# A block-wise FP4 quantiser on VectorE: the rounding constant from one ScalarE activation, in a decoder layer on one core

## What is computed

```
scale = max(max(|x| in the block) / 6, 1e-12)
xn    = x / scale
q     = grid[searchsorted(mid, |xn|)] * sign(xn) * scale
grid  = 0, 0.5, 1, 1.5, 2, 3, 4, 6      mid = 0.25, 0.75, 1.25, 1.75, 2.5, 3.5, 5
ffn   = down_q @ quant(silu(gate_q @ quant(x)) * (up_q @ quant(x)))
```

## Time and profile before

| what | value |
|---|---|
| time, median of 3 runs | 622.29 us (620.88 to 623.05) |
| the profiled execution's own time | 618.94 us |
| its span, first to last instruction | 617.2 us |
| PE busy | 549.6 us, 89% |
| DVE busy | 512.0 us, 83%, in 1444 instructions |
| ACT busy | 285.8 us, 46% |
| POOL busy | 177.5 us, 29% |
| mean granted clock of TensorE | 0.972 of full speed |

### The profile page before, as it was taken

The page is one execution under the profiler, slowest core; times in us unless marked ns, Lnnn a source line. Parts: engine busy times, 40 slices in busy tenths (PEclk is TensorE's granted clock), DMA queues, the critical chain, the costliest instruction groups (busy, mean ns, idle before and its releaser), DMA issues.

```text
span 617.2 us, 16429 instructions
## 1 busy us (share of the span) xinstructions
PE 549.6 (89%) x5724; PEld 351.0 (57%) x5724; DVE 512.0 (83%) x1444; ACT 285.8 (46%) x671; POOL 177.5 (29%) x251
## 2 busy tenths in 40 slices
PE   3686898889999999999999998998999998899875
PEld 2554354546565666666576656564665765455543
DVE  3587888787889989898999997567989996887894
ACT  1342145466454555545545455454455554444412
POOL 7014141423132414233242413141232424211211
PEclk9998699899999999999999998798999999998999
DMA  8366553445453554536263636345452635330000
GB/s 253 80 187 186 157 154 110 146 124 139 138 147 95 128 165 110 168 102 186 72 180 106 170 90 179 107 124 157 112 170 77 171 102 153 88 89 16 26 8 26
DMA packets 75933, 77.14 MB, mean 125 GB/s; under 512 B 13068, under 2 KB 67404, under 8 KB 75852
## 3 DMA queue, kind: packets, MB, share of 16 engines
q1 hardware_dynamic: 73612, 73.75, 42.1%
q10 hardware_dynamic: 2240, 2.35, 1.3%
HBM read 39.89 MB, written 27.00 MB: 108 GB/s over the span
## 4 chain that ended last, share of the span: by engine, by line
PE 50%; DVE 29%; issue 9%; ACT 4%; DMA 4%; SPq 2%; POOL 2%; DVEq 0%; POOLq 0%; ACTq 0%
PE misc L2248 16%; PE misc L2234 7%; DVE junk L1431 4%; PE prob L2173 4%; PE score L2164 3%; PE xpv L2223 3%; PE prob L2179 3%; PE apv L2211 3%; PE misc L2289 3%; DVE amax L1423 2%; DVE xden L1470 2%; DVE qt L1348 2%; PE misc L2276 2%; DVE qt L1338 2%; PE score L2140 2%
## 5 line engine op out<-in xcount | busy, mean ns | idle before, releaser
L1431 DVE CUSTOM_DVE_ANT_0 junk<-score,maskbias 112x375 bf16<-112x375 f32 x256 | 128.8, 541 | 27.3 <-PE score L2164 26.4
L932 ACT ACTIVATE xP<-prob 128x448 f32<-128x448 f32 (+1 forms) x192 | 94.0, 541 | 54.4 <-PE prob L2179 53.9
L2248 PE MATMUL misc<-wguT,xqT 128*128 128x352 f32 x224 | 80.8, 489 | 1.9 <-ACT xqT L892 1.1
L741 POOL TENSOR_TENSOR move_a<-mT,eye 128x448 bf16<-128x448 bf16 x32 | 36.3, 1152 | 73.6 <-ACT mT L892 73.6
L2164 PE MATMUL score<-xK,xQ 64*128 64x375 f16 x256 | 52.0, 339 | 5.8 <-DVE xmax L1431 2.6
L765 POOL TENSOR_TENSOR rstd<-veps,half 128x1 f32<-128x1 f32 (+1 forms) x44 | 28.2, 640 | 96.7 <-DVE veps L1506 96.7
L761 POOL TENSOR_TENSOR aattT<-anum,aden 128x224 f32<-128x224 f32 x16 | 11.1, 693 | 155.0 <-DVE aden L1470 107.9
L2248 PEld LDWEIGHTS misc<-wguT,xqT 128*128 128x128 f32 x224 | 39.4, 193 | 25.8 <-issue 9.0
L741 POOL TENSOR_TENSOR move_x<-mT,eye 128x448 bf16<-128x448 bf16 x32 | 33.1, 1040 | 72.0 <-ACT mT L892 72.0
L2223 PE MATMUL xpv<-xP,xV 128*32 128x112 f32 (+1 forms) x1536 | 51.5, 268 | 0.5 <-ACT xP L932 0.3
L2248 PE MATMUL misc<-xwvT_s,ctxT_s 128*128 128x256 f32 (+1 forms) x192 | 49.9, 392 | 1.5 <-ACT kcf L892 1.1
(11 more groups left out here) (158 smaller groups left out, 1095.5 us busy)
## 6 DMA issues: line engine op xcount, KB each, us to landing
xk_dram<-xk_parts SPq DMA_DIRECT2D x64, 192.0 KB, 3.2
xK<-xk_dram SPq DMA_DIRECT2D x16, 768.0 KB, 4.6
ctxT_s<-in_ctxT SPq DMA_DIRECT2D x15, 375.0 KB, 3.7
aq_dram<-aq_parts SPq DMA_DIRECT2D x64, 64.0 KB, 2.5
ak_dram<-ak_parts SPq DMA_DIRECT2D x64, 64.0 KB, 2.4
aQ<-aq_dram SPq DMA_DIRECT2D x16, 256.0 KB, 2.9
aK<-ak_dram SPq DMA_DIRECT2D x16, 256.0 KB, 2.9
xq_dram<-xq_parts SPq DMA_DIRECT2D x64, 64.0 KB, 2.1
```

Source lines behind the costliest of these rows:

```text
L741: pool.tensor_tensor(dst[:, big], mT[:, n, big].rearrange("p (j q) -> p j q", j=2).unsqueeze(2).to_broadcast([P, 2, GH, HS]), eye[:].unsqu ...
L932: act.activation(xP[0:KEYS[c], g % 2, c], prob[m][0:KEYS[c], 0:GH * S].rearrange("p (h q) -> p h q", h=GH), ACT.Exp).then_inc(probs.taken[ ...
L1431: dve.tensor_tensor_reduce(junk[:, m], score[m][0:S, 0:SC], maskbias[:], 1.0, -3.0e38, ALU.add, ALU.max, xmax[:, b.par, h // (2 * GH), h / ...
L2248: mm = pe.matmul(misc[m][0:rows_, 0:cols], actT(c), weightT(c), start=(c == 0), stop=(c == DT - 1))
```

## The change

The rounding constant no longer comes from two VectorE steps. After the product (k = 3) ScalarE writes the absolute value of it, times 2^22, as bf16 into `qt2`. VectorE then takes the maximum with a floor and adds or subtracts in the same instruction, so k = 4 is the addition, k = 5 the subtraction, k = 6 the product with the scale: seven steps for nine. The factor for ties moves into the product of k = 3, the sign is turned back in the last step. Step 4 waits for ScalarE (`turned()`), not for the step before it.

```
-                    done(dve.tensor_tensor(blocks(t1), blocks(v), spread(r), ALU.mult))
+                    done(dve.scalar_tensor_tensor(out=blocks(t1), in0=blocks(v), scalar=TIE, in1=spread(r), op0=ALU.mult,
+                                                  op1=ALU.mult))
                 elif k == 4:
-                    done(dve.tensor_scalar(t2.bitcast(U16), t1.bitcast(U16).rearrange("p (n k) -> p n k", k=2)[:, :, 1],
-                                           0x7F80, None, ALU.bitwise_and))
+                    done(dve.scalar_tensor_tensor(out=t1, in0=t2, scalar=FLOOR, in1=t1, op0=ALU.max, op1=ALU.add))
                 elif k == 5:
-                    done(dve.tensor_scalar(t2, t2, 1.0 / factor, ROUND * factor, ALU.max, ALU.mult))
-                elif k == 6:
-                    done(dve.scalar_tensor_tensor(out=t1, in0=t1, scalar=TIE * factor, in1=t2, op0=ALU.mult, op1=ALU.add))
-                elif k == 7:
-                    done(dve.tensor_tensor(t1, t1, t2, ALU.subtract))
+                    done(dve.scalar_tensor_tensor(out=t1, in0=t2, scalar=FLOOR, in1=t1, op0=ALU.max, op1=ALU.subtract))
                 else:
-                    last(dve.tensor_tensor(blocks(dst), blocks(t1), spread(s), ALU.mult))
+                    last(dve.scalar_tensor_tensor(out=blocks(dst), in0=blocks(t1), scalar=-factor, in1=spread(s), op0=ALU.mult,
+                                                  op1=ALU.mult))
```

The new calls on ScalarE:

```
+            def magnitude(lo, nb, ready):
+                cols = slice(lo * BLK, (lo + nb) * BLK)
+                act.activation(qt2[:, cols], qt1[:, cols], ACT.Abs, scale=STEP).then_inc(ready, 1)
+            def abs_weight(f):
+                act.wait_ge(c_quantw, 6 * f + 4)
+                magnitude(0, (min(2, GU - 2 * f) * D if f < 6 else I) // BLK, abs_ready[3])
+            def abs_x(b):
+                act.wait_ge(c_quant[0].sem, b.times(6, 4))
+                magnitude(I // BLK, D // BLK, abs_ready[0])
+            def abs_h(b, u):
+                act.wait_ge(c_quant[1 + u].sem, b.times(6, 4))
+                magnitude(u * (IH // BLK), IH // BLK, abs_ready[1 + u])
```

There are 50 of them: 8 for weights, 14 `abs_x`, 28 `abs_h`. Where they stand in ScalarE's list, in the slots:

```
                 exp_cross(i, p, 0, 2)
+                if f:
+                    abs_x(f)
                 exp_cross(i, p, 1, 2)
                 maxima(i, 0, "A.mT")
...
                     tanh(i, f, 1)
+                    abs_h(f, 0)
...
                 ctxk_hi(i, kv, 0)
+                if f:
+                    abs_h(f, 1)
                 ctxk(i, kv, 1)
```

and at four places that the prediction speaks of, in the ramp (the first two) and in the drain:

```
                 exp_cross(at[1], at[0], 1, 0)
+                abs_weight(4)
                 exp_cross(at[1], at[0], 0, 1)
...
                 exp_self(at[3], at[4], 3)
+                abs_weight(7)
+                abs_x(at[0])
                 exp_cross(at[3], at[2], 2, 1)
...
                 exp_self(at[14], at[15], 2)
+                abs_x(at[10])
                 exp_self(at[14], at[15], 3)
...
                 take(at[17], "X.xT", xqT[:], DT, P)
+                abs_h(at[12], 0)
+                abs_h(at[12], 1)
                 tanh(at[17], at[13], 0)
```

VectorE's list in the slots, between the last maxima:

```
                     quant_h(i, f, 1, 0)
-                    quant_h(i, f, 0, 4)
                 max_cross(i, c, 6)
...
                 moments(i, a, 0, "A.o", 0)
-                if f:
-                    quant_h(i, f, 0, 5)
                 moments(i, a, 0, "A.o", 1)
...
                 ctxk_lo(i, kv, 1)
                 if f:
-                    quant_h(i, f, 0, 6)
-                    quant_h(i, f, 1, 4)
+                    quant_h(i, f, 0, 4)
                 max_cross(i, c, 7)
```

In the ramp and the drain steps of the quantiser stand at somewhat other places between the same other calls. One other call is moved there:

```
                 quant_weight(1, 3)
+                bias_out()
                 quant_weight(1, 4)
                 quant_weight(1, 5)
                 quant_weight(1, 6)
-                quant_weight(1, 7)
-                quant_weight(1, 8)
                 quant_weight(2, 0)
-                bias_out()
                 invert(at[0], 0)
```

More of the change, by code:

```diff
@@ L1028, in ramp @@
                 q_hi(at[-1], at[1])
+                abs_weight(0)
                 k_hi(at[0], at[2])
@@ L1044, in ramp @@
                 q_hi(at[0], at[2])
+                abs_weight(2)
                 layernorm(at[0], 0, x1[:, at[0].par])
@@ L1053, in ramp @@
                 k_hi(at[1], at[3])
+                abs_weight(3)
                 exp_self(at[0], at[1], 2)
@@ L1264, in drain @@
                 exp_cross(at[15], at[14], 1, 1)
+                abs_x(at[11])
                 exp_cross(at[15], at[14], 0, 2)
                 exp_cross(at[15], at[14], 1, 2)
+                abs_h(at[10], 0)
                 exp_cross(at[15], at[14], 2, 0)
@@ L1275, in drain @@
                 maxima(at[15], 1, "X.mT")
+                abs_h(at[10], 1)
                 tanh(at[15], at[11], 0)
@@ L1315, in _, with quant_step @@
         def _(dve):
-            def quant_step(k, v, dst, factor, n, lo, nb, done, wait, last):
+            def quant_step(k, v, dst, factor, n, lo, nb, done, wait, turned, last):
                 a, s, r = (z[0:n, lo:lo + nb] for z in (qamax, qscale, qinv))
@@ L2349, in ramp @@
                 warm()
+                warm()
+                warm()
+                warm()
+                warm()
+                warm()
+                front(at[-2], at[0], "v")
+                mix_weight()
                 front(at[-2], at[0], "q")
                 ctx_k(at[-1], at[0], 0)
+                warm()
                 front(at[-2], at[0], "k")
```

240 lines of the change are left out of this document (101 added, 139 removed), and 12 rows, old and new, of tables (MISC_IN, MISC_OUT).

## The result

The changed kernel is slower: median 625.99 us of 12 runs against 621.45 us for the kernel before (12 runs), ratio 1.0076 with a 95% interval of 1.0046 to 1.0106. The forecast was 618.1 us and faster. 626.0 lies above its range (612.5 to 624.5). Single executions of one program scatter by up to 1% either way (616.5 to 624.6 before, 620.4 to 632.9 after), so I read places from the profiles and the size from the ratios. Executions more than 1.5% above the fastest of their kernel, here 630.3 and 632.9 us after, are left out of the ratios and means.

A forecast was written before the change was run, and what follows sets the result against it. PE was taken to bound a slot, busy 32.49 of 33.50 us. Slots -8.6, ramp +4.3, drain +0.9 and clock -0.8 summed to -4.2, giving 618.1 us against the median 622.29; range 612.5 to 624.5.

The forecast's parts named there:

- Slots, forecast -8.6: Slots: -6.2 and -0.8 from PE's wait for the maxima, -1.6 from the wait before `turn_xq`.
- 0.78 against a wait of 0.77: PE's wait goes to about nothing: Slots, before X.mT: three removed DVE instructions, 0.78 us, cancel PE's wait for maxima; -6.2, and -0.8 in slot 9.
- Rival C: Slots: `abs_x` ahead of an exponential delays `move_a`, losing 0.4 us in each of nine slots; 622.5 us, chance 0.18.
- Sum +4.3: Ramp: `bias_out` +2.2, `abs_weight(4)` +0.6, `abs_weight(7)` with `abs_x(0)` +1.5, other calls zero.
- upper 5: Ramp: upper bound in us on its total delay; the lower bound was 0.
- the exponential starts at 85.5, not 84.96: Ramp: `abs_weight(4)` ahead of an exponential delays it by 0.6 us.
- rival D: Clock: longer ramp waits bring clock falls of 1.65 us each; three more give 623.9, four 625.5; chance 0.13.
- Drain, forecast +0.9: Drain: `abs_h(12, 0)` and `abs_h(12, 1)` ahead of tanh of tile 13 add 0.9 us; smaller terms cancel.
- the clock, -0.8: Slot 9: half of a 1.65 us loss to low clock goes, since the wait ahead shrinks; -0.8 us.
- B: Ramp: delays don't last, as later PE waits for DVE shrink; both clock effects go; 613 us, chance 0.22.
- E: ScalarE: absolute value needs table switches, two 1.28 us loads for each of 50 calls, over 60 us; chance 0.02.

The follow-up runs named there:

- the doubling: Changed kernel with each of a slot's three ScalarE calls done twice, the extra result going to an unread buffer; ratio 1.0156 to the kernel before.
- bias_back: Changed kernel with `bias_out` moved back behind `quant_weight(2,0)`; ratio 1.0024 to the kernel before.
- abs_later: Changed kernel with `abs_weight(4)`, `abs_weight(7)` and `abs_x(0)` put behind the exponential pairs they split or precede; ratio 1.0034 to the kernel before.
- two_back: Changed kernel with `bias_out` back and `abs_weight(4)`, `abs_weight(7)`, `abs_x(0)` behind their exponential pairs; ratio 0.9972 to the kernel before.
- abs4_later: Changed kernel with only `abs_weight(4)` put behind the exponential pair it splits; ratio 1.0022 to the kernel before.
- the fills: Extra warm products in TensorE's ramp waits: 20 in the changed kernel (1.0147), 8 in two_back (0.9995), 8 in the kernel before (1.0106).
- before_fill: Kernel before with 8 more warm products ahead of `project_self(at[-1], at[0])`; ratio 1.0106 to the kernel before.
- bias_early: Kernel before with `bias_out` alone moved ahead of `quant_weight(1,4)`; ratio 1.0113 to the kernel before.
- abs7_later: Changed kernel with only `abs_weight(7)` and `abs_x(0)` put behind the exponential pair they precede; ratio 1.0087 to the kernel before.

## Why the prediction was wrong

**Slots, forecast -8.6, came -4.8: the right wait, and about half the size.** The step that failed is "0.78 against a wait of 0.77: PE's wait goes to about nothing". The distances between starts in the earlier trace rows were taken as time that would be saved. Shown: 0.25 of it was. The other two removed instructions covered a wait of DVE for PE's score and the pause between statistics and aggregation. Nine times 0.25 is 2.3 where 7.0 was forecast. The wait ahead of `turn_xq` went whole, 2.3 us in nine slots (forecast 1.6); ScalarE's delay, which I had let eat part of it, found slack, and the doubling shows that in the later slots 0.4 more finds it too. Rival C fell. By the distance of X.mT it is 0.53 a slot, 4.8 us.

**Ramp, forecast +4.3, measured +11.9.** The step that failed is "Sum +4.3", with "upper 5": it adds up three places and has no term for the clock, whose own term, -0.8, looks at slot 9 alone. The three places were the right ones. `bias_out`: 2.5 for 2.2, since a subtraction took 1.10 us for the 0.69 assumed. `abs_weight(7)`, `abs_x(0)`: 1.4 for 1.5. `abs_weight(4)`: the step "the exponential starts at 85.5, not 84.96" failed; it is the second exponential of the pair at 83.25 that is held up, and PE is 1.7 late where 0.6 was forecast. That is 5.6.

The other 6.3 us of this profile are what the forecast gave to rival D, the clock: half for 38 us of the ramp instead of 18. D was given 0.13. Its figure with four more falls, 625.5, is the nearest to the 626.0 measured, but that is luck in part, since it stands on the slots' gain as forecast, which was put 3.8 too high.

What is shown: mending these places takes about their own delay off the time. By the ratios bias_back wins 3.2 us (its wait was 2.5), abs_later 2.6 (3.1), two_back 6.5 (5.6), each uncertain by 2.5 to 3 us; by the rests they win 1.4, 1.5 and 4.2, each uncertain by half a us or more. Taken over many executions the clock's part is smaller than in the two profiles. The places of this account, -4.8 in the slots, +5.6 in the ramp and +1.5 in the drain, make +2.3. The mean spans differ by 5.3, of which the estimate gives +3.0 to the clock and +2.3 to the rest. So the kernel would be slower by its places alone, and the clock more than doubles it. That the longer waits cause the lower clock is argued, from where the stretches stand and from abs_later; which stretch belongs to which wait stays open. abs4_later and the fills show that one avoided at a place can come some microseconds later.

**Drain, forecast +0.9, and the clock, -0.8.** From 566 us to the end the lateness rises by 1.5. Tanh of tile 13 followed the eviction ahead of it by 2.35 us (599.69 to 602.04), before by 1.98 (594.08 to the earlier trace rows), so the two calls cost 0.4 and not 0.9, the first being done while DVE made the second product. Ahead of that `abs_x(13)`, which the forecast did not price, stands in front of tanh of tile 12: this tanh followed its eviction by 2.60 us (592.15 to 594.75), before by 1.98 (587.51 to 589.49), 0.6 more. Tile 13's `turn_xq` then waited 0.70 for DVE and not 0.33, 0.4 more. I made no experiment on the drain. From 200 to 566 us the lateness falls by 7.2: 4.8 are the slots, the other 2.4 are put down to the falls at 377 and 561 us, which this execution does not have. The one at 377 goes with the change: all three profiles with the old quantiser have it (before, before_fill, and bias_early at 388), of the fifteen with the new one only abs7_later (at 385). So the forecast's half of a fall in slot 9 was nearly a whole one. The one at 561 is in two of the three and in two of the fifteen.

**The sum.** In the two profiles -4.8 (slots), +11.9 (ramp), +1.5 (drain) and some -2.4 (clock behind the ramp) make +6.2. The forecast had -4.2; the 10.4 between them are the ramp's clock (6.3), its places (1.3), the slots (3.8) and the drain (0.6), less 1.6 of clock behind the ramp.

**Rivals B and E.** B fell: the ramp's delays were there at 200 us to the tenth. E fell: one table load in the run,

```profile
L1016 ACT ACTIVATE qt<-qt 128x352 bf16<-128x352 f32 x28 | 13.9, 496 | 4.3 <-DVE qt L1386 3.6
...
L1016 ACT ACTIVATE qt<-qt 128x512 bf16<-128x512 f32 x5 | 3.1, 630 | 9.3 <-DVE qt L1386 9.3
...
L901 ACT ACT_TABLE_LOAD x1 | 1.3, 1283 | 2.8 <-issue 2.8
```

which is what the Trainium skill, "ScalarE: Activation LUTs", section "Table sets: the hidden batching unit", says of abs. The Trainium skill, "ScalarE: Activation LUTs", section "What ACT_TABLE_LOAD costs", gives an activation with immediate scale and bias 186 ns and 0.833 ns a column. By that page an estimate is 479 ns at 352 and 612 at 512 columns; the rows have 496 and 630.

## What to carry to other kernels

When a step is taken from a queue, its length is saved only if the next instruction was waiting for the engine. Look at what the next one would wait for instead (another engine's product, its own operand), and price the smaller of the two. A new call on a shared in-order queue costs what it waits for and not only what it lasts (0.99 and 0.63 us here, inside a pair of exponentials): put it behind the work that is ready. And while a pipeline fills, a longer wait of TensorE may be paid more than once: in the two profiles the clock behind the longer waits was half for longer, which is not shown as a rule. Mending the order of four calls brought 6.5 us here by the ratio; the two instructions saved per block brought 4.8 in the slots. When a time does not move, look at the mean granted clock of each execution before you call a gain nothing.

## What was not expected of the hardware

Statistics and their aggregation on VectorE start 0.47 us apart whether a 0.23 us instruction stands between them or none, in all nine slots. Two VectorE instructions of one kind and size took 0.69 and 1.10 us in the ramp (the steps at 47.59 and 48.31). A product on GpSimd ran from 47.82 to 48.86; the first had started ahead of it, the second started during it and ended 0.55 behind its end. In bias_back the subtraction of the same step, with no GpSimd product beside it, took 0.69. And the warm products put into the wait at 50 us kept the clock full over that wait, but in all three kernels that have them a stretch at half clock came 4 to 7 us later than the one they replaced.
